# Attention scores from three bf16 parts instead of two fp32r parts, V weighted eight heads at a time, and a new order of steps

## What is computed

```python
x = layernorm(x + attention0(x))   # 16 heads of 8, causal, softmax, output projection
x = layernorm(x + moe0(x))         # 8 experts, top 2, relu, hidden size 256
x = layernorm(x + attention1(x))   # 16 heads of 8, no mask, biases
x = layernorm(x + moe1(x))         # 15 experts, top 3, gelu(g) * h, and a shared expert
# in both attentions, for each batch and head:
s = (q @ k.T) * 8 ** -0.5
o = softmax(s) @ v                 # q, k, v: 256 x 8
```

## Time and profile before

| | us |
|---|---|
| median of 3 runs | 1208.55 |
| the three runs | 1205.19, 1208.55, 1209.41 |
| span of the profiled execution, first to last instruction | 1058.9 |
| the profiled execution's own time | not among the runs listed |
| PE busy in the span | 906.3 (86%) |
| mean granted TensorE clock | 0.927 of full |

### The profile page before, as it was taken

How to read it: one execution, slowest core, us unless ns; L and a number is a source line. 1 busy time by engine, 2 the same in 40 slices (tenths; PEclk the granted TensorE clock), 3 DMA queues, 4 the chain that set the end, 5 groups by cost and what they waited for, 6 DMA issues and landing times.

```text
span 1058.9 us, 23206 instructions
## 1 busy us (share of the span) xinstructions
PE 906.3 (86%) x7486; PEld 763.1 (72%) x7486; DVE 679.9 (64%) x2209; ACT 549.4 (52%) x1320; POOL 444.0 (42%) x688
## 2 busy tenths in 40 slices
PE   5899988995999996998999896899898999789910
PEld 4788878884899985766888665676666789688810
DVE  3467755673644475987655566888875565378863
ACT  1356654562655564666766474567556655334300
POOL 7000100054500075477200375325776157377774
PEclk9699998997999998999999897999989999989965
DMA  4557564555468433364667333323444789888421
GB/s 78 103 107 193 114 142 101 135 135 133 106 178 204 125 68 59 53 125 85 144 182 191 66 57 58 51 35 56 87 90 130 216 264 326 280 247 270 122 64 53
DMA packets 111752, 138.49 MB, mean 131 GB/s; under 512 B 12275, under 2 KB 86033, under 8 KB 111633
## 3 DMA queue, kind: packets, MB, share of 16 engines
q1 hardware_dynamic: 100241, 114.97, 45.9%
q0 software_dynamic: 10240, 20.99, 7.9%
q10 hardware_dynamic: 1152, 1.05, 0.6%
HBM read 70.25 MB, written 42.48 MB: 106 GB/s over the span
## 4 chain that ended last, share of the span: by engine, by line
PE 49%; DMA 20%; issue 8%; POOL 7%; DVE 7%; SPq 6%; ACT 2%; POOLq 0%; ACTq 0%; DVEq 0%
DMA QK<-parts 10%; PE bank_O L1132 5%; PE bank_N L1224 5%; DMA G<-yd,ypos 5%; PE bank_FH L1212 4%; POOL xs L877 4%; PE bank_S L1087 4%; PE bank_T L1110 3%; PE bank_S L1083 3%; PE bank_S L1085 3%; PE bank_T L1114 3%; SPq L736 2%; PE bank_T L1112 2%; PE bank_M L1056 2%; DMA QK<-mrow 2%
## 5 line engine op out<-in xcount | busy, mean ns | idle before, releaser
L1298 DVE TENSOR_REDUCE mp<-bank_S 128x3 f32<-128x384 f32 (+1 forms) x512 | 304.2, 620 | 133.9 <-PE bank_S L1087 91.7
L948 ACT ACTIVATE P<-bank_T 128x384 f32<-128x384 f32 (+1 forms) x512 | 260.9, 543 | 90.0 <-PE bank_T L1114 58.2
L891 POOL DMA_INDIRECT G<-yd,ypos x160 | 155.2, 970 | 76.1 <-issue 47.3
L877 POOL DMA_INDIRECT xs<-X,ypos x160 | 155.9, 974 | 48.7 <-issue 43.6
L1132 PE MATMUL bank_O<-P,V 128*32 128x256 f32 (+1 forms) x2048 | 128.8, 371 | 1.4 <-ACT P L948 1.0
L1083 PE MATMUL bank_S<-QK 96*128 96x256 f32 x512 | 112.4, 322 | 18.5 <-DMA QK<-parts 8.9
L1110 PE MATMUL bank_T<-QK 128*128 128x256 f32 x512 | 110.8, 322 | 10.6 <-ACT P L948 6.1
L828 POOL TENSOR_TENSOR rstd<-mv,half 128x2 f32<-128x2 f32 x48 | 9.6, 200 | 261.4 <-DVE mv L1351 261.1
L1085 PE MATMUL bank_S<-rmat 128*128 128x256 f32 x256 | 91.7, 358 | 22.3 <-DMA QK<-parts 21.6
L1083 PEld LDWEIGHTS bank_S<-QK 96*128 96x128 f32 x512 | 79.5, 201 | 35.8 <-DVE mp L1298 20.5
L1087 PE MATMUL bank_S<-QK 96*128 96x128 f32 (+1 forms) x512 | 104.7, 292 | 0.0
(11 more groups left out here) (171 smaller groups left out, 1753.3 us busy)
## 6 DMA issues: line engine op xcount, KB each, us to landing
QK<-parts SPq DMA_DIRECT2D x192, 128.0 KB
QK<-wtab SPq DMA_DIRECT2D x76, 257.0 KB, 3.9
W<-w_in SPq DMA_DIRECT2D x46, 321.0 KB, 4.0
QK<-xs SPq DMA_DIRECT2D x38, 256.0 KB, 4.3
yd<-P SPq DMA_DIRECT2D x38, 256.0 KB, 3.9
xs<-zeros SPq DMA_DIRECT2D x17, 512.0 KB, 8.1
xp<-xs SPq DMA_DIRECT2D x22, 256.0 KB, 4.1
yd<-yb SPq DMA_DIRECT2D x22, 256.0 KB, 4.0
```

The lines of the kernel that those rows point to most:

```text
L877: pool.indirect_dma_start(xs[g % 2], bass.IndirectOffsetOnAxis(ypos[L][:, 2 * b + blk, k:k + 1], 0), X[:, 2 * b + blk, :], None).then_inc( ...
L891: pool.indirect_dma_start(G[i][:, blk, k, :], None, yd[g], bass.IndirectOffsetOnAxis(ypos[L][:, 2 * b + blk, k:k + 1], 0))\
L948: act.activation(P[:, (h // 4) % 2, h % 4, 0:n], bank[("T0", "T1")[h % 2]][:, 0:n], ACT.Exp, scale=SCALE)\
L1298: dve.tensor_reduce(mp[:, a % 2, 0:n, h], bank[("S0", "S1")[h % 2]][:, 0:n * w] .rearrange("p (a c) -> p a c", a=n), AX.X, ALU.max).then_i ...
```

## The change

Queries and keys go to three bf16 parts. ACT writes the first (`qk_hi`), DVE what is left in fp32 (`qk_rest`, which frees bank M), ACT the second (`qk_mid`), DVE the third (`qk_low`). `parts` holds six slots. SP writes all of them to a DRAM tensor `stk` in one copy (`spread_parts`), then reads them back with three copies (`stack`), for all 16 heads at once, into one of three buffers QK of 16 heads in bf16. Six products of parts are stacked on the same 96 partitions. The row maxima become three bf16 parts (rows 96 to 98), cut out of the fp32 words by reading their upper halves (`top_half`), the reduction negates directly, and `max_T` is a bf16 matmul. The mask matmuls are bf16.

`weigh_V` stays fp32 and takes eight heads: two heads share a 32-column tile. Each weight is 18 columns wide, one head's V and ones beside zeros for the other, and four matmuls a tile add up. P has 12 head slots. O is evicted twice a batch, `O_T` makes four transposes a batch, `O_norm` runs once a batch on both halves.

The numbers in `PRM` are all new, and with them the order. In the last expert stage the first pages now wait for `scores_T` of batch NA - 3 instead of NA - 2, the first weights for all of NA - 2 instead of its first half.

```diff
-VW = HD + 1
+VW = 2 * (HD + 1)
+PAIR = VW
+PSLOTS = 12
+BURST = 8
+BURSTS = NH // BURST
...
+def before_slot(a, h):
+
+    m = NH * a + h - PSLOTS
+    return ("weigh_V", m // NH, m % NH // BURST)
+
+
+def p_slot(a, h):
+    return (NH * a + h) % PSLOTS
...
-        S = (0.35, 0.245)[L]
+        S = (0.30, 0.235)[L]
...
-        add(t + qk[2], "DVE", (0.72, 0.9)[L], 0.1, "qk_lo", a, after=[("qk_hi", a)], frees="M")
-        add(t + PRM["v"][ph], "PE", 0.44, 0.25, "v", a, after=x + [("weigh_V", a - 3, 3)], bank="M")
+        add(t + qk[2], "DVE", (0.72, 0.9)[L], 0.1, "qk_rest", a, after=[("qk_hi", a), ("qk_low", a - 1)], frees="M")
+        add(t + qk[2], "ACT", 0.63, 0.1, "qk_mid", a, after=[("qk_rest", a)])
+        add(t + qk[2], "DVE", 0.63, 0.1, "qk_low", a, after=[("qk_mid", a)])
+        add(t + qk[2], "SP", 0.68, 3.4, "spread_parts", a, after=[("qk_low", a), ("stack", a - 2)])
...
+        add(t, "SP", 2.03, 4.6, "stack", a, after=[("spread_parts", a), ("scores_T", a - 3, 15)])
...
+                add(e, "PE", S, 0.25, "scores_T", a, h, after=[("max_rows", a, u)], bank=("T0", "T1")[h % 2])
+                add(e + 0.4, "ACT", (0.51, 0.62)[L], 0.1, "exp", a, h, after=[("scores_T", a, h), before_slot(a, h)], frees=("T0", "T1")[h % 2])
...
+            add(e + wv[0], "PE", (1.58, 1.99)[L], 0.3, "weigh_V", a, u,
+                after=[("exp", a, h) for h in heads] + [("v_keep", a), ("O_T", a - 1)], bank="O")
+            add(e + wv[1], "ACT", 0.4, 0.1, "keep_O", a, u, after=[("weigh_V", a, u)], frees="O")
...
-        parts = sb("parts", [D, 2, 2, T], F32R)
-        QK = [sb(f"QK{i}", [D, NH // 2, 2, T], F32R) for i in range(4)]
-        VPAD = NH * VW + 32 - VW
-        V = [sb(f"V{i}", [D, 2, VPAD]) for i in range(3)]
-        P = sb("P", [D, 2, 4, 2 * T])
-        OT = sb("OT", [D, 4, T])
+        parts = sb("parts", [D, 2, 3, T], BF16)
+        rest = sb("rest", [D, 2, T])
+        QK = [sb(f"QK{i}", [D, 2, NH, T], BF16) for i in range(3)]
+        V = [sb(f"V{i}", [D, 2, VW // 2 + NH * VW]) for i in range(3)]
+        P = sb("P", [D, PSLOTS, 2 * T])
+        OT = sb("OT", [D, BURSTS, T])
...
-            def stack(a, u):
-                c = 2 * a + u
+            def spread_parts(a):
                 sp.wait_ge(lo_done.sem, lo_done.all(a))
-                if a < 2:
-                    sp.wait_ge(cleared.sem, 1 + 3 * c)
-                    if c == 0:
+                if a >= 2:
+                    sp.wait_ge(stacked[(a - 2) % 3].sem, stacked[0].all((a - 2) // 3))
+                sp.dma_start(stk[a % 2].rearrange("i p t -> p i t"), slots(parts[:, :, :, :])).then_inc(spread[a % 2].sem, DMA)
+
+            def stack(a):
+                sp.wait_ge(spread[a % 2].sem, spread[a % 2].all(a // 2))
+                if a < 3:
+                    sp.wait_ge(cleared.sem, 1 + 3 * a)
+                    if a == 0:
                         sp.wait_ge(cleared_dve.sem, 2)
                 else:
-                    sp.wait_ge(st_ps.sem, st_ps.at(a - 2, 8 * u + 8))
-                p = parts[64 * u:64 * u + 64, :, :, :].bitcast(F32).rearrange("p s i t -> p (s i) t")
-                for i, pair in enumerate((p[:, 0::2, :], p[:, 0::3, :], p[:, 1:3, :])):
-                    sp.dma_start(QK[c % 4][HD * i:HD * i + HD, :, :, :].bitcast(F32), pair).then_inc(stacked[c % 4].sem, DMA)
+                    sp.wait_ge(st_ps.sem, st_ps.all(a - 3))
+                for row, n in ((0, 3), (3, 2), (5, 1)):
+                    pair = stk[a % 2].rearrange("i (d h) t -> (i d) (h t)", h=NH).rearrange("(s r) c -> r s c", s=2) if n == 3 else \
+                        stk[a % 2].rearrange("(m i) (d h) t -> (i d) m (h t)", m=3, h=NH)[:, 0::2, :] if n == 2 else \
+                        stk[a % 2].rearrange("i (d h) t -> d i (h t)", h=NH)[:, 0::5, :]
+                    sp.dma_start(QK[a % 3][row * HD:(row + n) * HD, :, :, :].rearrange("r s h t -> r s (h t)"), pair)\
+                        .then_inc(stacked[a % 3].sem, DMA)
...
+            def qk_mid(a):
+                act.wait_ge(rest_done.sem, rest_done.all(a))
+                act.activation(slots(parts[:, :, :, :])[:, 1::3, :], rest[:, :, :], ACT.Copy).then_inc(mid_done.sem, 1)
...
             def exp(a, h):
                 act.wait_ge(st_ps.sem, st_ps.at(a, h + 1))
-                if h % 4 == 0 and 4 * a + h // 4 >= 2:
-                    act.wait_ge(o_ps.sem, 4 * a + h // 4 - 1)
+                if NH * a + h >= PSLOTS:
+                    _, before, u = before_slot(a, h)
+                    act.wait_ge(o_ps.sem, o_ps.at(before, u + 1))
                 n = 3 * D if a < NB else 2 * T
-                act.activation(P[:, (h // 4) % 2, h % 4, 0:n], bank[("T0", "T1")[h % 2]][:, 0:n], ACT.Exp, scale=SCALE)\
+                act.activation(P[:, p_slot(a, h), 0:n], bank[("T0", "T1")[h % 2]][:, 0:n], ACT.Exp, scale=SCALE)\
                     .then_inc(exped.sem, 1)
 
-            def keep_O(a, g):
-                act.wait_ge(o_ps.sem, o_ps.at(a, g + 1))
-                if g == 0 and a >= 1:
+            def keep_O(a, u):
+                act.wait_ge(o_ps.sem, o_ps.at(a, u + 1))
+                if u == 0 and a >= 1:
                     act.wait_ge(oT_ps.sem, oT_ps.all(a - 1))
-                act.activation(OT[:, g, :], bank["O"][:, 0:T], ACT.Copy).then_inc(o_kept.sem, 1)
+                act.activation(OT[:, u, :], bank["O"][:, 0:T], ACT.Copy).then_inc(o_kept.sem, 1)
...
                 m.then_inc(qk_ps.sem, 1)
-                held["M"] = lo_done.sem, lo_done.all(a)
+                held["M"] = rest_done.sem, rest_done.all(a)
...
             def scores(a, h):
                 k = ("S0", "S1")[h % 2]
                 S = free(k)
-                c = 2 * a + h // 8
-                Q, K = QK[c % 4][0:96, h % 8, 0, :], QK[c % 4][0:96, h % 8, 1, :]
+                Q, K = QK[a % 3][0:96, 0, h, :], QK[a % 3][0:96, 1, h, :]
                 if a == 0 and h == 0:
-                    pe.wait_ge(warmed.sem, 2)
-                if h % 8 == 0:
-                    pe.wait_ge(stacked[c % 4].sem, stacked[c % 4].all(c // 4))
+                    pe.wait_ge(const_in.sem, CONST_LOADS * DMA)
+                if h == 0:
+                    pe.wait_ge(stacked[a % 3].sem, stacked[a % 3].all(a // 3))
                 if a >= NB:
                     for qb in range(2):
                         m = pe.matmul(S[:, qb * T:(qb + 1) * T], Q[:, qb * D:(qb + 1) * D], K)
                 else:
-                    pe.matmul(diagonal(S), identr, mask_q, start=True, stop=False, skip_group_check=True)
+                    pe.matmul(diagonal(S), identb, mask_q, start=True, stop=False, skip_group_check=True)
                     for qb, (o, n) in enumerate(((0, D), (D, 2 * D))):
...
-                    m = pe.transpose(M[0:NH, qb * D:(qb + 1) * D],
-                                     neg[:, u, qb, :, :].rearrange("p i h -> p (i h)").bitcast(F32), ident)
+                    m = pe.matmul(M[0:3 * NH // 2, qb * D:(qb + 1) * D], top_half(mp[:, a % 2, u, qb, :, :].rearrange("p i h -> p (i h)")), identb)
...
-            def weigh_V(a, g):
+            def weigh_V(a, u):
                 O = free("O")
-                pe.wait_ge(exped.sem, exped.at(a, 4 * g + 4))
-                if g == 0:
+                if a == 0 and u == 0:
+                    pe.wait_ge(cleared_O.sem, 1)
+                pe.wait_ge(exped.sem, exped.at(a, BURST * (u + 1)))
+                if u == 0:
                     pe.wait_ge(v_kept.sem, v_kept.all(a))
                 for kb in range(2):
-                    for j in range(4):
-                        h = 4 * g + j
-                        w = V[a % 3][:, kb, h * VW:h * VW + 32]
-                        if a >= NB or kb == 0:
-                            o, x = O[32 * j:32 * j + 32, 0:T], P[:, g % 2, j, kb * T:(kb + 1) * T]
-                        else:
-                            o, x = O[32 * j:32 * j + 32, D:T], P[:, g % 2, j, T:T + D]
-                        m = pe.matmul(o, w, x, start=(kb == 0), stop=(kb == 1), skip_group_check=True)
+                    for half in range(2):
+                        for j in range(BURST // 2):
+                            h = BURST * u + 2 * j + half
+                            w = V[a % 3][:, kb, h * VW + (VW // 2 if half == 0 else 0):][:, 0:VW]
+                            q = 0 if a >= NB else kb * D
+                            x = P[:, p_slot(a, h), kb * T:kb * T + T - q]
+                            m = pe.matmul(O[32 * j:32 * j + VW, q:T], w, x, start=(kb == 0 and half == 0), stop=(kb == 1 and half == 1),
+                                          skip_group_check=True)
                 m.then_inc(o_ps.sem, 1)
-                held["O"] = o_kept.sem, o_kept.at(a, g + 1)
-
-            def O_T(a, blk):
+                held["O"] = o_kept.sem, o_kept.at(a, u + 1)
+
+            def O_T(a):
                 N = free("N")
                 pe.wait_ge(o_kept.sem, o_kept.all(a))
-                for g in range(4):
```

(39 more changed lines are left out.)

201 lines of the change are left out of this document (92 added, 109 removed), and 17 rows, old and new, of the table PRM.

## The result

The change makes the kernel slower: 1261.66 us (median of 4 runs, 1254.03 to 1266.82) against 1208.36 us for the kernel before in the same comparison, a ratio of 1.042 [1.036, 1.047]. 1163 was forecast.

What follows compares the result with a forecast made beforehand. PE was taken as the bound, at 86% of the span, with DVE as close in layer 1. Layer 0 -34, layer 1 -7, buffers -5, start +4, third part +2, order -5 gave -45 us: 1163.5 us, range 1125 to 1205.

Steps and rivals of the forecast that it cites:

- I convert 0.85: Layer 0 attention: 40 us less PE work gives 34 us of time; layer 1's 18 us, at 0.4, gives 7.
- I give the re-tuned order ... another 5: The order searched anew gains 5 us, against stretches where PE idles 23 of 250 and 22 of 200 us.
- rival C: Attention: parts' chain and stack come late, PE waits; +31 us, 1240 us; chance 0.13.
- Layer 0 tile: Layer 0 scores: bf16 saves 0.05 us on each of 512 tiles, 26 us of PE (0 to 34).
- Rival A: Score tiles: bf16 streams no faster than fp32r; gain only 22 us, 1187 us; chance 0.15.
- Third part: DVE gains a subtraction, ACT a copy; net DVE +0.2 to +0.6 us a batch, 2 us lost in layer 1.
- Start: First batch: half-microsecond steps and a second DMA hop delay the first score by 4 us (2 to 10).
- Deeper buffers: Three whole-batch QK buffers cut waits for scores_T to free a buffer; gain 5 us (0 to 15).
- The stage after 850 us: Last expert pages and gathers, untouched by the edit; forecast fails if this span changes by more than 10 us.
- The 149.7 us: Time taken to lie around the profiled span, 1208.55 - 1058.9, and added unchanged to the forecast span of 1014 us.
- Rival B: DVE and score banks take over, DVE starving behind bursts of eight, 20 us in layer 1; 1189 us; chance 0.13.
- Rival D: The order searched anew with cheaper steps also closes layer 1's slack, another 30 us; 1133 us; chance 0.14.

Runs made afterwards that it cites:

- E1: The kernel before, unchanged, run again: 1058.73 against 1055.3 us, ratio 1.002; profiled span 1060.1 us.
- E4: The changed kernel, unchanged, run again where the kernel before takes about 1055 us: 1089.69 against 1056.67 us, ratio 1.031.
- E15: The changed kernel with four xT buffers, its order searched anew with measured landings and operation costs: 1207.42 against 1209.43 us for the kernel before, ratio 0.996.
- E18: E15 run again as a second comparison: 1202.29 against 1210.3 us for the kernel before, ratio 0.996.
- E13: The changed kernel with xT in four buffers instead of two, each load a batch earlier: 1228.59 against 1209.43 us for the kernel before, ratio 1.018.
- E5: The changed kernel's operations put step by step in the order of the kernel before, without planning again: 1209.34 us, ratio 1.146 to the kernel before.
- E14: The changed kernel with its order searched anew for measured landings and operation costs, xT buffers as they were: 1242.9 against 1209.43 us for the kernel before, ratio 1.029.
- E12: The changed kernel, unchanged, once more in the slower condition: 1253.92 against 1209.43 us for the kernel before, ratio 1.037.
- E16: The kernel before, unchanged, profiled in the slower condition: ratio 0.999 against 1210.3 us.
- E6: As E5, but V weighted in groups of four as before: 1196.19 us, ratio 1.132 to the kernel before.
- E17: The kernel before with xT in four buffers, each load a batch earlier: ratio 1.001 against 1210.3 us.
- E7: As E5, but parts copied SBUF to SBUF by six copies without the DRAM tensor, from two parts buffers: 1320.62 us, ratio 1.250 to the kernel before.
- E9: The changed kernel with SP's bulk copies between a batch's spread and stack moved behind the stack: 1285.96 against 1221.04 us for the kernel before, ratio 1.049.
- E11: The changed kernel with the 21 page-buffer clearing copies issued by POOL instead of SP: 1265.43 against 1221.04 us for the kernel before, ratio 1.036.
- E2: The changed kernel with the PRM numbers of the kernel before: 1112.88 us, ratio 1.053 to the kernel before.

## Why the prediction was wrong

**The step that failed** is the one from PE's savings to time: "I convert 0.85", "0.4", and "I give the re-tuned order ... another 5". PE's operations became shorter, by more than was summed, but the conversion was below zero: PE's busy time fell by 51 us and its idle time rose by 81 (E1, E4), and the best order that was run ends at 0.996 (E15, E18). Its mechanism is near rival C, which got 0.13: the parts come late. C priced it at +31 us, and the loss in span is 30 us in E4's condition, 53 us of time in the result's; that the size is so near is luck, since C's terms are others. C blamed the chain from matmul to stack alone; late xT, which the prediction named only as something that queues on SP, added more to PE's waits in E4 (27.7 us against 16.3) and is worth about 2 of the 3.7 points (E13). Its stated sign, PE waiting for the stacked parts or the clock dropping between 50 and 400 us, is what E4 shows (0.91 for 1.00 and 0.95).

**The terms.**
- Layer 0 tile: taken 0.05 us, measured 0.366 - 0.275 = 0.091, 47 us of PE instead of 26 and above the upper bound of 34. The closest pair of starts of before was no bound: bf16 streams at 0.11 us for 256 columns (105.00 to the next start, 105.11), and its weights load in 104 ns, where fp32r took about 200.
- Layer 1 tile: taken 0.01, measured 0.045, 23 us instead of 5. Rival A is refuted.
- V: taken 0.23 a join, measured 0.15 in layer 0 and 0.28 in layer 1, 14 us for 15. One `O_T`: its four transposes take about 0.44 us (707.43 to 707.89 in E4 is 0.46), where four took 0.36 to 0.39, so some 10 us are saved for 12.
- These are some 94 us; PE's busy time fell by 51. Over the span the granted clock fell from 0.94 (E1) to 0.90 (E4): idle time costs a second time, as in the stretch at 0.50 above. An estimate of full-speed work, 907.9 x 0.94 - 856.6 x 0.90 = 83 us, is near the sum. The prediction had no term for that.
- Third part: right in its items. DVE takes 716 ns and ACT 629 ns a batch, with 0.77 us of `O_norm` for 1.09, which nets to 0.4 us for the 0.2 to 0.6 taken. DVE's total changed by only 2 us, so the 2 us put down for it in layer 1 aren't contradicted.
- Start: the first score came at 23.69 instead of 17.88 us, 5.8 for the 4 taken (range to 10). The first exponential came 0.3 us later, so it cost nothing.
- Deeper buffers: wrong in sign. The stack's waits rose by 16 us. SP's waits for QK buffers, over both forms of `scores_T`, did fall, from 258 us (E1) to 195 (E4), but its wait for DVE's last part rose from 57 to 145.
- The order: not +5 but the decisive term. It was fitted to a stack that lands in 4.6 us and takes about 10 (E4's start, E5, E14's effect on that wait); yet E14, fitted to 9.6, gained only 0.8 of a point, so this alone isn't the loss.
- The stage after 850 us: "nothing there was costed". It takes 12 us more in E4 than in E1, and 33 us more in E12 than in E16, of 30 and 48 us between the spans. The forecast's own condition for failing is met in both. Attention itself loses about the same in either condition, 18 and 16 us.
- The 149.7 us: an addition with a wrong name. The profiled run shown was from a condition in which the kernel takes 1059 us. It shifted no sign, since the result is a ratio, but the forecast in microseconds rested on it. A span and a median that differ by 14% should have been read as two conditions, not as time outside the span.
- Rival B: DVE didn't take over (busy as before, 63% in E4), but starving beside long bursts is in part real. Its sign, DVE's idle time before the layer 1 `row_max`, grew from 36.6 us to 46.2; PE's added waits for DVE's maxima and ACT's weights are 31 of the 88 us; and E6 puts 13 us on the bursts in the old order. Rival D (the new order closes slack) is refuted for the order as it was.

**What is shown and what is not.** Shown: the xT loads cost about 2 points (E13), and only the changed kernel (E17); a new order with four xT buffers ends level with before or 0.4% below it (E15, E18). That this order wins by the measured landings is argued from the waits that went, not shown alone. Shown not to be the cause: the DRAM hop, as against direct copies (E7); the place and the queue of the bulk copies (E9, E11); that the numbers of the order were changed at all (with the old ones, E2, it is slower still). Open: the stack's share, since in E14, which took its wait away, others took its place. Open: what makes the last expert stage longer. In the first condition it is the order and not the operations; in the second the standstills are a part (ACT waits 82 us on remote there in E18, 60 in E16), but no run separates them. Open too: whether E15 would be clearly faster in the condition of E1; it didn't run there.

## What to carry to other kernels

When a kernel's order is searched against a table of costs, the landing time of a new transfer is as much part of the change as its instructions: measure it in the new shape before searching. Here the table had 4.6 us for a stack that takes 10. In a stretch where an engine is 91 to 99% busy, its transfers can be just early enough; when its work gets 10% shorter, look first at which transfer is then last, and give that one its own buffers. Here that was worth more than the new costs alone (2 points against 0.8). Before blaming a copy in whose issue a queue is held, move it and see whether the hold moves on to the next one. Compare a profiled span with the listed times before adding anything to it.
